# Where the dense layer's second product stands in TensorE's row: four pieces spread through the last head's slot, or one block behind it

## The reference

```
xn = layernorm(x)
x + attention(xn) + ( silu(xn Wg + bg) * (xn Wu + bu) @ Wd + bd ) + experts(xn)
```

## Time and profile before

| | |
|---|---|
| median of 3 runs | 1788.02 us (1785.41 to 1789.31) |
| the profiled execution's own time | 1786.72 us |
| its span, first to last instruction | 1785.0 us |
| mean granted TensorE clock | 0.96 |
| TensorE matmul busy | 1556.2 us, 87% |
| VectorE, ScalarE, GpSimd busy | 1110.1, 960.3, 958.5 us |
| start of the transposes L1712, unit after unit | 44.9 us apart, in some units 46.6 |

### The profile page before, as it was taken

The page is one execution under the profiler, slowest core; times in us unless marked ns, Lnnn a source line. Parts: engine busy times, 40 slices in busy tenths (PEclk is TensorE's granted clock), DMA queues, the critical chain, the costliest instruction groups (busy, mean ns, idle before and its releaser), DMA issues. The chain is left out here.

```text
span 1785.0 us, 42002 instructions
## 1 busy us (share of the span) xinstructions
PE 1556.2 (87%) x14000; PEld 1132.5 (63%) x14096; DVE 1110.1 (62%) x4508; ACT 960.3 (54%) x1776; POOL 958.5 (54%) x886
## 2 busy tenths in 40 slices
PE   3899957899999999999999999999999999999867
PEld 2566635666666666666666666666666666666657
DVE  3344347676766666666666666666666666666612
ACT  0555405555555555555555555555555555555641
POOL 4444416555555555555555555555555555555620
PEclk8899968999999999999999999999999999999989
DMA  6445530111111111111111111111111111111026
GB/s 183 156 154 166 167 110 8 32 38 37 37 37 37 37 37 37 37 37 37 37 37 37 37 37 37 37 37 37 37 37 37 37 37 37 37 37 37 8 69 227
DMA packets 151611, 105.09 MB, mean 59 GB/s; under 512 B 63336, under 2 KB 145688, under 8 KB 151576
## 3 DMA queue, kind: packets, MB, share of 16 engines
q1 hardware_dynamic: 143128, 96.27, 18.3%
q10 hardware_dynamic: 8448, 8.39, 1.4%
HBM read 64.45 MB, written 40.16 MB: 59 GB/s over the span
## 5 line engine op out<-in xcount | busy, mean ns | idle before, releaser
L1089 POOL TENSOR_TENSOR sumxy<-xy 128x1024 f32<-128x1024 f32 x128 | 241.2, 1909 | 0.0
L1319 DVE TENSOR_REDUCE bmax<-q_bank 128x32 f32<-128x512 f32 (+3 forms) x512 | 218.5, 482 | 4.6 <-PE q_bank L1551 2.4
L1412 DVE SCALAR_TENSOR_TENSOR mw<-sumxy,c,ex 128x1024 f32<-128x1024 f32 x128 | 170.2, 1331 | 71.3 <-ACT ex L1194 71.3
L1179 ACT ACTIVATE pts<-k_bank 128x512 f32<-128x512 f32 (+2 forms) x384 | 179.1, 494 | 49.2 <-PE k_bank L1587 46.2
L1551 PE MATMUL q_bank<-ko,qo 96*128 96x512 bf16 (+3 forms) x512 | 143.2, 307 | 43.6 <-DVE bmax L1319 43.6
L1342 DVE TENSOR_REDUCE lmax<-q_bank 128x8 f32<-128x512 f32 x64 | 43.4, 690 | 208.9 <-PE q_bank L1573 208.9
L1113 POOL TENSOR_TENSOR cw<-cw,mw 128x1024 f32<-128x1024 f32 x64 | 156.8, 2450 | 22.6 <-ACT mw L1200 20.0
L1533 PE MATMUL f_bank<-xt,wfg 128*128 128x128 f32 x1024 | 159.0, 283 | 1.8
L1533 PE MATMUL f_bank<-xt,wfu 128*128 128x128 f32 x1024 | 159.3, 278 | 0.0
L1533 PEld LDWEIGHTS f_bank<-xt,wfu 128*128 128x128 f32 x1024 | 145.1, 192 | 10.1
L1194 ACT ACTIVATE ex<-sumxy,nmax 128x1024 f32<-128x1024 f32 x128 | 146.6, 1146 | 0.8 <-issue 0.8
(11 more groups left out here) (233 smaller groups left out, 3593.3 us busy)
## 6 DMA issues: line engine op xcount, KB each, us to landing
qo<-s_qs SPq DMA_DIRECT2D x192, 64.0 KB, 2.2
ko<-s_ks SPq DMA_DIRECT2D x192, 64.0 KB, 2.2
s_qs<-parts SPq DMA_DIRECT2D x8, 768.0 KB, 3.8
s_ks<-parts SPq DMA_DIRECT2D x8, 768.0 KB, 6.2
s_v<-vo SPq DMA_DIRECT2D x8, 544.0 KB, 3.0
vv<-s_v SPq DMA_DIRECT2D x32, 136.0 KB, 2.3
xin<-in_L_attn_x_dram SPq DMA_DIRECT2D x8, 512.0 KB, 7.1
s_xt<-xT SPq DMA_DIRECT2D x8, 512.0 KB, 7.1
```

The source lines that it names most:

```text
L1089: done("sum_done", g_.tensor_tensor(sumxy[:, h, :, :], xy[:, 0, h, 0:XK, None].broadcast_to([P, XK, KEYS]), xy[:, 1, h, None, :].broadcast ...
L1179: last = s.activation(pts[:, h, OFFS[j]:OFFS[j] + n], bank[:, 0:n], ACT.Exp)
L1319: last = v.tensor_reduce(bmax[:, i, h, 0:n], Q.bank(job)[:, o:o + n * BLK].rearrange("p (n j) -> p n j", j=BLK), AX.X, ALU.max)
L1412: done("mw_done", v.scalar_tensor_tensor(mw[:, h, :], sumxy[:, h, :, :].rearrange("p a b -> p (a b)"), c8[:, h, 7:8], ex[:, h % 2, :], ALU ...
```

## The change

The call of `mlp_down` leaves slot 3 of TensorE's step; all four parts are called in a row behind the slot and ahead of the transposes. The same instructions are issued on every engine, and no wait or semaphore is added but the one that goes along with part 2. Only TensorE's row differs.

```
                             if h < 3:
                                 up_rows(t, "ugu"[h], (0, 1, 1)[h], part)
-                            else:
-                                mlp_down(t, part)
                             if n and part < 3:
                                 queries(n, h, part)
                             if part == 2 and h < HG - 1:
                                 head_shifts(t, h + 1)
+                    for part in range(4):
+                        mlp_down(t, part)
                     transposed_weights(t)
```

## The result

The changed kernel takes 1793.45 us (median of 6 runs, 1790.36 to 1795.02); the kernel before, on the same chip, 1788.41 (6 runs, 1785.41 to 1790.29). The ratio is 1.0028, with a 95% interval of 1.0018 to 1.0038: slower by 5.0 us, a difference that this kernel's measurement can tell. Forecast were 1792, range 1784 to 1800.

The account below looks back on a forecast made before the run. TensorE bounds the kernel, its transposes waiting 2.0 us a unit for GpSimd's product. Chain 1.2, last unit 0.4 and clock 2.5 sum to +4.1 us on 1786.72 (1790.8), or 1792.1 against the median 1788.02; predicted 1792, range 1784 to 1800.

Parts of the forecast that it names:

- The uncovered wait: In TensorE's slot 3, moving the down matmuls uncovers the 256-column score matmul's wait for VectorE's reduction: 2.72 us.
- The two chains: From the end of `cand` to the transposes: VectorE and TensorE 6.23 us, GpSimd 6.15; +0.04 us per unit after corrections.
- the 0.05 that they give back: Transposes to the next group take 0.97 us behind running matmuls, 1.02 behind a stall: 0.05 less per unit.
- the 0.01 for a slow start: Work behind the late score matmul may follow it later: bounded by 0 and 0.10 us, taken as 0.01 per unit.
- The last unit: There the down matmuls had covered ScalarE's reading of the keys banks: +0.4 us once, between 0 and 1.
- The clock: Behind the longer stall, over keys and down matmuls, 9.5 lower-clock losses instead of 8, 1.69 us each: +2.5 us.
- The proportion between a stall's length and the number of losses: In the main stage, 8 losses scaled by stall length, 2.72 / 2.16, give 10.1; 9.5 was taken.
- A: No change: GpSimd's chain still ends last before the transposes, lower clock as often as now; 1788 us within 1.5; 24%.
- B: Lower clock over keys job and down product in every second unit, 15 losses instead of 8: +12 us, above 1801; 12%.
- C: Faster: the stall without transposes is too short a quiet, so the 8 main-stage clock losses go: 1776 us; 6%.
- D: Small gain: TensorE reaches the transposes before GpSimd, and clock losses fall out better by two: 1784 us; 8%.

## Why the prediction was right

**The uncovered wait.** It was put at 2.72 us from stream to stream, with the matmul 1.99 us behind the end of `cand`. The trace has 1.99 and a record of 2.55, for which 2.6 was expected. The run with the score matmul behind the block shows that this wait ahead of the block, and not the block, is what costs.

**The two chains.** Forecast were 6.23 us through VectorE and TensorE against 6.15 through GpSimd. Measured is 6.23. The run with the longer block shows that TensorE's end now decides at full rate. Of the unit's increase I expected 0.04 us and found 0.015: the transposes start 0.07 later instead of 0.08, the 0.05 that they give back when no stall stands ahead was right, and the 0.01 for a slow start behind the stalled matmul was not there (544.77 to 544.89 is 0.12 to the next job). In sum 0.5 instead of 1.2 us.

**The last unit.** 0.4 us forecast, 0.2 measured over the last two.

**The clock.** This was the largest term, +2.5 us of 4.1, and only guessed between two ends. The direction and the place were right: the losses moved from L1611 onto the down product. The size was low for the profiled execution: one loss more in the 28 like units, but 4.4 us up to the second transposes, which my count, taken from the middle of the stage, left out. The twelve low stretches are at the upper end of the 8 to 12 named. In the medians the change is 5.0 us; by the traces the chain is about 0.6 of it and the rest clock, but there is one trace of each kernel, so how the 5.0 of the medians divide is argued and not shown. That the time came out within 1.5 us is then partly luck: the chain was put too high (1.6 with the last unit, against 0.6) and the clock too low (2.5, against some 4.4), and the two errors partly cancel. The proportion between a stall's length and the number of losses, from which the 2.5 was taken, is not borne out either: with the same stall of 2.55 us there were nine losses in 28 units, and 16 where the unit was 0.43 us longer.

**The rivals.** No change (A) lies just below the measured interval. B, a loss in every second unit, comes true only where the block is made 0.43 us longer. C, that the losses go because no transposes prolong the stall any more, is refuted: a stall of 2.72 us with matmuls behind it was followed by the lower clock in nine of 28 units, one of 2.16 with transposes behind it in eight. The Trainium skill's "TensorE: Matmul & The Clock Gate", Part 4: PE-mode transpose, says that a transpose doesn't count as busy for the clock the way a matmul does. By it the quiet would have shrunk here from 3.02 to 2.72 us, but the losses did not become fewer. These counts alone don't tell whether a transpose counts; it is the transposes at a granted clock of 1.00 in the earlier trace rows that disagree with the page. D is excluded by the sign.

## What to carry to other kernels

A product with no wait of its own that stands among work that waits is cover; before it is moved, ask what it stands in front of, and add the wait that comes out to the chain behind it, from the point at which both chains part. TensorE's slack of 2 us a unit was worth far more here than the place of this product: independent work moved into it won 83 us, and a change that looks nearly free beside such slack can cost its full size once the slack is used, as it did here with 90.6 us. Where a stall can't be filled with use, it is worth trying to split it: here two short ones were better than one long one.

## What the runs showed of the hardware that was not expected

A stall of 2.00 us (2.55 in the changed kernel), repeated each 45 us, cost more through the clock than the change did through its chain: 13.5 us and 15 us in 28 units. Matmuls without use in it took 17.5 us off the kernel before and 20.6 off the changed one. Splitting about the same waiting into 0.69 and 1.49 us, with about 2.7 us of matmuls between, did nearly as well (14.8 us), though no unit's full-clock time changed. And lengthening the unit by 0.43 us, with the stall as it was, brought seven losses more in 28 units.
